# Attention a: another order of the work inside a step, on TensorE first and on the four engines that feed it

## The chip, the cores and the metric

The kernel runs on one core of one Trainium2 chip. The metric is the device time of one execution in microseconds (us). Before the change it is 5544.91 us, the median of three runs (5527.25 to 5550.4).

## The reference, cut to what matters

Four blocks run one after the other on x of shape 32 x 256 x 128: attention a, a mixture of experts, attention b, the mixture of experts again. The change touches attention a alone:

```python
q, k, v = heads of (layernorm(x) @ W_qkv.T + b_qkv)      # 16 heads of 8
scores = q @ k^T * 128 ** -0.5                           # 256 x 256 for each batch and head
masked = the largest 76 scores of each row, -inf elsewhere
out = softmax(masked) @ v
x = x + out @ W_out.T + b_out
```

The top 76 of 256 in each row are the costly part. The kernel finds a threshold for each row: three counting passes over the scores steer a guess to within a few ranks, and a short exact search ends it.

## The kernel before

**Groups and steps.** Attention a handles 64 groups. A group is 8 heads of one batch, so each batch has two. The code issues one `step(t, b, u)` after another (`schedule`, a software pipeline written out by hand): u = t mod 4, an even step is the first of its batch bb = t // 2. The middle of it is a hardware loop (`Fori`) whose body is four steps, so every fourth step ends with the loop's branch. In step t the engines work on different groups:

- TensorE makes the raw scores of group t+1 (`score`, L641, and the first two heads of t+2 at the end, `first_scores`). For groups t-3 and t-2 it makes the transposed scores less the row's maximum (`below_max`, L668), adds a huge negative number where a score is under its threshold (`remove`, L675), and multiplies the exponentials by the values (`weigh`, L689).
- VectorE (DVE) moves the scores from three rotating banks `S` to SBUF, taking the row maximum (`evac`, L961). For group t-1 it takes the sixteen largest values under the upper threshold (`largest`, L976 to L989); for t-2 it picks the threshold (`picks`), checks it (`check_flags`, L1035) and, where a row failed, searches again (`redo`). It normalises the sums (`normalise`, L1025, L1027).
- ScalarE (ACT) counts in three passes of 16 (`count`, L845), takes the exponentials (`exponentials`, L831) from the two banks `PT` to `pT`, and moves projections and sums out of PSUM.
- GpSimd (POOL) moves the guesses between passes (`move`, L479 to L481), computes the scores under the threshold (`outsiders`, `gone`, L493), and two powers (`front`, L453 and L454, and `guess`, L459). SyncE's queue issues the copies and the transposing DMA of each group's negated maxima.

**The order on each queue.** TensorE's step has four parts, d = 0 to 3. Part d handles a pair of heads (`PAIRS`: heads 2,3 then 4,5 then 6,7 of group t-3, then 0,1 of group t-2). `free_bank(t + 1, n + 1)` waits until DVE has evacuated the bank that the next two heads of scores need; then two `below_max`, two `score` and two `remove` are interleaved, twice; then come the projections of the batch ahead, and last `weigh` of the same pair. ACT's step has nine parts, h = 0 to 8, each about five counts; the exponentials of a pair stand ahead of h = 1, 3, 5 and 7. DVE's step has eight parts, one for each head.

**The shared banks.** The projections, the moments, the transposes of the sums and the flags go through two more banks, M0 and M1. `USES` lists the order in which their users take turns, and `m0_before` and `m1_before` turn an entry into a semaphore count: a user waits until the user before it has been read out.

Of the kernel before, what the change touches and what calls it, by code (L numbers as in the profile page):

```python
# [5 lines left out]
P = 128  # L6
# [50 lines left out]
def build(nc, x, W_qkv, b_qkv, W_out, b_out, Wq, Wk, Wv, Wp, pos, gate_w, gate_bias,  # L57
# [7 lines left out]
    with ctx:  # L65
# [307 lines left out]
        def wait(eng, sm, v):  # L373

            if not (isinstance(v, int) and v <= 0):
# [5 lines left out]
        USES = ({"v": 0, "xT": -1, "q0": -1, "q1": -1, "k": -1, "qn": -1, "gram": -1, "qtok": -1, "mom": -1},  # L381
                {"f0": 1, "ktok": -1, "n0": 2, "oT": 2, "f1": 1, "y": 2, "n1": 1})

        def before(m, b, what):

            order = USES[m]
            first = sum(lag == -1 for lag in order.values())
            if not isinstance(b, int):
                return b * len(order) + first - sum(max(lag, 0) for lag in order.values()) + list(order).index(what)
            n = first  # L390
            for c in range(b + 1):
# [26 lines left out]
        PAIRS = ((3, 2), (3, 4), (3, 6), (2, 0))  # L418

# [15 lines left out]
        with nc.Block() as block:  # L435
            @block.gpsimd
            def _(pool):
# [31 lines left out]
                def step(t, b, u):  # L469
# [49 lines left out]
                    if even and runs(bb, 0, BATCH):  # L519
                        wait(pool, s["m0c"], m0_before(bb, "v") + 1)  # L520
# [37 lines left out]
            def _(pe):  # L558
# [43 lines left out]
                def moments(n):  # L602
                    use0(n)
                    for h in range(HALVES):
                        last = nc.tensor.matmul(M0[:, 0:P], ktok[:, h, :], ktok[:, h, :], start=(h == 0), stop=(h == HALVES - 1))
                    last.then_inc(s["m0"], 1)
# [20 lines left out]
                wait(pe, s["m1c"], 1)  # L627
                for n, f in enumerate((moments, q_rows, spreads)):
                    f(5 + n)
# [25 lines left out]
                def step(t, b, u):  # L655
# [23 lines left out]
                    def weigh(g, v, h):  # L679
# [4 lines left out]
                        if h == 0:  # L684
                            wait(pe, s["oc"], g)
                            pe.wait_ge(s["vput"], bb)
# [7 lines left out]
                    def turn_sums():  # L694
                        wait(pe, s["oc"], t - 2)
                        use1(m1_before(bb, "n0" if even else "n1"))
                        for i in range(HALVES):
                            for c in range(2):
                                last = nc.tensor.transpose(M1[:, (i * 2 + c) * P:(i * 2 + c + 1) * P], osum[:, c, i * P:(i + 1) * P], ident[:, :])
                        last.then_inc(s["m1"], 1)  # L700

                    def turn_o():
                        pe.wait_ge(s["on"], 2 * (bb - 1))
                        use1(m1_before(bb, "oT"))
                        for i in range(HALVES):
                            last = nc.tensor.transpose(M1[:, i * P:(i + 1) * P], onrm[:, i, :], ident[:, :])
                        last.then_inc(s["m1"], 1)

                    def project_o():
                        use1(m1_before(bb, "y"))  # L710
# [6 lines left out]
                    for d in range(4):  # L717
# [3 lines left out]
                        ahead = d < 3 and runs(t, -1)  # L721
                        n = 2 * d + 2
                        if ahead:
                            free_bank(t + 1, n + 1)
                        if runs(g):
                            wait(pe, s["turned"], TURNED * (g + 1))
                            wait(pe, s["pt"], 8 * g + a)
                        for k in range(2):
                            if runs(g):
                                below_max(v, a, k)  # L730
                                below_max(v, a + 1, k)
                            if ahead:
# [8 lines left out]
                        if even:  # L741
                            if d == 0 and runs(bb, 0, BATCH):
                                values(m0_before(bb, "v"))
                            if d == 1:
                                if runs(t, 2):
                                    judged()
                                if front:
                                    turn_x(bb + 1, m0_before(bb, "xT"))
                            if d == 2 and front:
                                project(1, m0_before(bb, "q1"))  # L750
                                k_rows(m1_before(bb, "ktok"))
                            if d == 3 and runs(t, 3):
                                turn_sums()
                        else:
                            if d == 0:
                                if tail:
                                    turn_o()
                                if front:
                                    wait(pe, s["m1c"], m1_before(bb, "ktok") + 1)
                                    moments(m0_before(bb, "gram"))  # L760
                            if d == 1:
                                if runs(t, 2):
                                    judged()
                                if front:
                                    spreads(m0_before(bb, "mom"))
                            if d == 2 and tail:
                                project_o()
                            if d == 3 and runs(t, 3):
                                turn_sums()
                        weigh(g, v, a)  # L770
                        if even and front:
                            if d == 1:
                                project(0, m0_before(bb, "q0"))
                            if d == 2:
                                project(2, m0_before(bb, "k"))
                            if d == 3:
                                queries(m0_before(bb, "qn"))
                        if not even and front and d == 0:
                            wait(pe, s["m0c"], m0_before(bb, "qn") + 1)
                            q_rows(m0_before(bb, "qtok"))  # L780
                    if even and front:
                        wait(pe, s["m0c"], m0_before(bb, "k") + 1)
                    if runs(t, -2):
                        first_scores(t + 2, u + 2)
# [4 lines left out]
            def _(act):  # L789
# [32 lines left out]
                take_qn(4)  # L822
                own.end()
# [10 lines left out]
                def step(t, b, u):  # L834
# [18 lines left out]
                    for h in range(9):  # L853
                        if h % 2 == 1:
                            late, a = PAIRS[h // 2]
# [8 lines left out]
                        if h == 0 and even and runs(bb, 0, BATCH):  # L864
                            take_v(bb, m0_before(bb, "v"))
                        if even and front:
# [4 lines left out]
                            if h == 7:  # L871
# [4 lines left out]
                        if not even and h == 1 and runs(bb, 2, BATCH):  # L876
                            wait(act, s["m1"], m1_before(bb, "oT") + 1)
                            nc.scalar.copy(oT[:, :], M1[:, 0:T]).then_inc(s["m1c"], 1)
# [6 lines left out]
            def _(dve):  # L885
# [35 lines left out]
                def take_g(n):  # L921
                    wait(dve, s["m0"], n + 1)
                    V.tensor_tensor(gram[:, :], M0[:, 0:P], mask_bd[:, :, :].rearrange("p h d -> p (h d)"), ALU.mult).then_inc(s["m0c"], 1)

                def take_mom(b, n):
                    wait(dve, s["m0"], n + 1)
                    dve.sem_inc(s["gate"], 1)
                    wait(dve, s["m0c"], n)
# [9 lines left out]
                take_g(5)  # L938
                take_qr(6)
                take_mom(0, 7)  # L940
                own.end()

                def step(t, b, u):
# [76 lines left out]
                    def normalise():  # L1020

                        n1 = m1_before(bb - 1, "n1") if even else m1_before(bb, "n0")
# [21 lines left out]
                    for h in range(8):  # L1044
# [10 lines left out]
                        if h == 0 and runs(t, 4):  # L1055
# [3 lines left out]
                        if front and even and h == 6:  # L1059
                            take_k(m1_before(bb, "ktok"))  # L1060
                        if front and not even:
                            if h == 1:
                                take_g(m0_before(bb, "gram"))
                            if h == 2:
                                take_qr(m0_before(bb, "qtok"))
                            if h == 4:
                                take_mom(bb + 1, m0_before(bb, "mom"))
                        if h == 6 and not even and tail:
# [849 lines left out]
```

## Time and profile before

| | |
|---|---|
| profiled execution | 5548.73 us |
| span of its core | 5547.0 us |
| TensorE (PE) busy | 4738.9 us, 85% |
| weight loads (PEld) busy | 3322.2 us, 60% |
| VectorE (DVE) busy | 4094.9 us, 74% |
| ScalarE (ACT) busy | 3148.7 us, 57% |
| GpSimd (POOL) busy | 2516.4 us, 45% |

Attention a fills about the first 2810 us. Of the 40 slices of the span, the first twenty show a granted TensorE clock of mostly 5 or 6 tenths, the others 9 or more. A row of the waits names the engine and the instruction that stood still, what released it, and then the total, the number of times and the longest. A row of the timeline gives the start, the duration, the engine, the line, what is written and read, how many were merged (x4), and in brackets how long the engine had been idle and what ended that.

### The profile page before, as it was taken

To read this page: it belongs to the slowest core of one execution; us is meant where nothing else is said; L and a number is where in the kernel's file an instruction comes from. 1 tells how busy PE (TensorE), PEld (TensorE's weight loads), DVE (VectorE), ACT (ScalarE), POOL (GpSimd) and SP (SyncE) were. 2 spreads that over 40 slices of the span, in tenths; PEclk is the share of its full clock that TensorE was granted. 3 is DMA by queue.
4 is the path that set the end of the run, shared out by engine and by line. 5 is a ranking of instruction groups with operands and counts; after the bars stand their busy time and mean duration, and the time that the engine had idled before them with its cause. 6 is when DMAs were issued, how large, how long until landed. Compare 5 with 4: busy or idle time off the path is not lost. (4 is left out here: it accounts for less than half of the span.)

```text
span 5547.0 us, 121740 instructions
## 1 busy us (share of the span) xinstructions
PE 4738.9 (85%) x34686; PEld 3322.2 (60%) x34686; DVE 4094.9 (74%) x14487; ACT 3148.7 (57%) x10145; POOL 2516.4 (45%) x3026
## 2 busy tenths in 40 slices
PE   4578788788786887887889999989999998999998
PEld 2244444444443444444468888866666666888887
DVE  3788888888887888888958888855555554788886
ACT  3587777677775777777622222257667776222222
POOL 0465555565554555656644444421111111444444
PEclk6566665565665566667589999999999999999999
DMA  2000000000000000000023443410000000434344
GB/s 67 10 13 10 10 13 10 10 13 9 10 13 7 13 10 10 13 10 12 7 58 81 84 85 81 89 24 10 10 10 12 10 10 9 92 77 91 78 87 98
DMA packets 358589, 188.51 MB, mean 34 GB/s; under 512 B 190691, under 2 KB 346886, under 8 KB 358150
## 3 DMA queue, kind: packets, MB, share of 16 engines
q1 hardware_dynamic: 358150, 183.55, 16.4%
q8 instruction: 167, 2.74, 0.2%
q14 instruction: 272, 2.23, 0.1%
HBM read 147.04 MB, written 11.01 MB: 28 GB/s over the span
## 5 line engine op out<-in xcount | busy, mean ns | idle before, releaser
L845 ACT ACTIVATE junk<-SS,nt 128x256 bf16<-128x256 f32 x3072 | 1515.4, 502 | 188.4 <-POOL nt L481 113.3
L493 POOL TENSOR_SCALAR gone<-SS,mid 128x256 bf16<-128x256 f32 x1024 | 1193.0, 1180 | 664.3 <-DVEq L1039 533.2
L1206 POOL TENSOR_TENSOR f_hid<-f_g_m,f_cbs 128x256 f32<-128x256 f32 x1024 | 743.4, 726 | 853.2 <-DVE f_g_m L1451 660.6
L1306 ACT ACTIVATE f_th<-bank 128x256 f32<-128x256 f32 x1088 | 417.1, 383 | 1149.0 <-PE bank L1237 1149.0
L1236 PE MATMUL bank<-f_xTf,wgT 128*128 128x256 f32 x2176 | 692.3, 400 | 54.3 <-DVE f_g_m L1451 38.6
L668 PE MATMUL bank<-q4x,k4x 32*128 32x256 f32 x2048 | 526.2, 603 | 224.4 <-DVE SS L961 186.9
L1852 DVE TENSOR_REDUCE nmxb<-bank 128x2 f32<-128x512 f32 x512 | 330.1, 688 | 474.6 <-PE bank L1624 474.6
L1237 PE MATMUL bank<-f_xTf,wuT 128*128 128x256 f32 x2176 | 651.5, 381 | 0.0
L1268 PEld LDWEIGHTS bank<-wdT,f_hid 128*128 128x128 f32 x4096 | 601.5, 191 | 66.9 <-POOL f_hid L1206 12.5
L1268 PE MATMUL bank<-wdT,f_hid 128*128 128x128 f32 x4096 | 629.6, 276 | 10.5 <-POOL f_hid L1206 10.4
L845 ACT ACTIVATION_READ_ACCUMULATOR junk<-SS,nt 128x1 f32 x3072 | 599.5, 195 | 0.0
L689 PE MATMUL bank<-pT,vaug 128*32 128x256 f32 x2048 | 436.2, 572 | 136.1 <-ACT pT L831 133.5
L1443 DVE SCALAR_TENSOR_TENSOR f_g_s<-f_th,bank 128x256 f32<-128x256 f32 x1088 | 452.0, 415 | 107.1 <-ACT f_th L1306 87.5
L976 DVE SCALAR_TENSOR_TENSOR zt<-SS,hi_t 128x256 f32<-128x256 f32 x1024 | 481.9, 511 | 59.3 <-issue 28.4
L961 DVE TENSOR_SCALAR_CACHE_REDUCE SS<-bank 128x256 f32<-128x256 f32 x1024 | 386.9, 416 | 170.3 <-PE bank L641 157.8
L1451 DVE TENSOR_TENSOR f_g_m<-f_g_s,bank 128x256 f32<-128x256 f32 x1088 | 457.1, 420 | 74.9 <-DVE f_g_s L1443 3.7
L641 PE MATMUL bank<-k,q 32*128 32x256 f32 x2048 | 465.9, 559 | 30.3 <-DVE SS L961 30.1
L1743 ACT ACTIVATE probb<-bank,nmxb 128x256 f32<-128x256 f32 x1024 | 440.6, 494 | 78.7 <-DVE nmxb L1852 78.7
L668 PEld LDWEIGHTS bank<-q4x,k4x 32*128 32x128 f32 x2048 | 219.7, 261 | 415.5 <-DVE SS L961 236.0
L1553 POOL TENSOR_TENSOR q<-qrow,mask_h 128x1024 f32<-128x1024 f32 x64 | 137.2, 2144 | 715.8 <-DMA qrow<-q_rows 649.6
L1237 PEld LDWEIGHTS bank<-f_xTf,wuT 128*128 128x128 f32 x2176 | 416.3, 191 | 57.3
L831 ACT ACTIVATE pT<-bank 128x512 f32<-128x512 f32 x512 | 276.1, 592 | 277.8 <-PE bank L675 277.7
(233 smaller groups left out, 8134.9 us busy)
## 6 DMA issues: line engine op xcount, KB each, us to landing
f_cbs<-f_shares SPq DMA_DIRECT2D x512, 256.0 KB, 5.8
q4x<-q SPq DMA_DIRECT2D x64, 256.0 KB, 2.3
k4x<-k SPq DMA_DIRECT2D x64, 128.0 KB, 2.1
qrow<-q_rows SPq DMA_DIRECT2D x512, 8.0 KB
q_rows<-qTb SPq DMA_DIRECT2D x32, 128.0 KB, 1.7
out_dram<-xres SPq DMA_DIRECT2D x4, 1024.0 KB, 9.3
q4x<-nmx_rows SPq DMA_DIRECT2D x128, 4.0 KB
f_shares<-f_combT SPq DMA_DIRECT2D x64, 32.0 KB, 1.4
```

What stands on the lines that cost most here:

```text
L493: last = pool.tensor_scalar(gone[:, h % 4, i, :], SS[:, (u - lag) % 4, c, :], mid[:, (u - lag) % 4, c:c + 1], 0.0, ALU.subtract, ALU.min)
L641: last = nc.tensor.matmul(S[h % 3][:, i * T:(i + 1) * T], q4[rows(h), par, 2 * (u % 2) + h // 4, i * P:(i + 1) * P], k4[rows(h), par, u % ...
L668: nc.tensor.matmul(PT[h % 2][:, k * T:(k + 1) * T], k4x[rows(h), v, k * P:(k + 1) * P], q4x[rows(h), v, h // 4, :], start=True, stop=False)
L845: nc.scalar.activation(junk[:, c % 2, :], SS[:, uu % 4, c, :], ACT.Sign, bias=bias(c), accum_out=acc[:, k, uu % 4, c:c + 1]).then_inc(s["s ...
L976: n = own.mark(V.scalar_tensor_tensor(zt[:, i, :], SS[:, z, c, :], hi_t[:, y, c:c + 1], SS[:, z, c, :], ALU.is_le, ALU.mult))
L1206: pool.tensor_tensor(hid[:, e % NBUF, :], g_m[:, e % NBUF, :], cbs[:, par, e, :], ALU.mult).then_inc(s["hid"], 1)
L1236: nc.tensor.matmul(g[:, 0:T], wgT[:, e, :], xTf[:, par, :], start=True, stop=True)
L1237: nc.tensor.matmul(g[:, T:2 * T], wuT[:, e, :], xTf[:, par, :], start=True, stop=True).then_inc(s["gu"], 1)
L1268: last = nc.tensor.matmul(Y[par][h][:, 0:D], src[:, h * P:(h + 1) * P], wdT[:, e, :], start=(e == 0), stop=(e == NBLK - 1))
L1443: n = own.mark(V.scalar_tensor_tensor(g_s[:, e % 3, :], th[:, e % 3, :], 1.0, g[:, 0:T], ALU.add, ALU.mult))
L1451: V.tensor_tensor(g_m[:, e % NBUF if e < EB else NBUF, :], g_s[:, e % 3, :], g[:, T:2 * T], ALU.mult).then_inc(s["gm"], 1)
L1743: last = nc.scalar.activation(probb[:, u % 4, i, :], S[u % 4][:, i * T:(i + 1) * T], ACT.Exp, bias=nmx[:, u % 4, i:i + 1], scale=1.0)
```

## The change

TensorE: in each part d the scores of the next group come first, as four `score` pairs in a row, and `below_max` and `remove` follow by themselves. `weigh` follows another table, `SUMS`, and handles the pair of the part before. `turn_sums` moves from the end of step t to part 0 of the next step. Of the projections, `values` moves from part 0 of the even step to the end of the odd step before, behind `first_scores`; `turn_x` from part 1 to part 0; the moments (`gram`) from part 0 of the odd step to the end of the even one, and to bank M1; `turn_o` from part 0 to part 1, and to bank M0; `queries` goes behind `first_scores`.

ACT: the exponentials stand ahead of h = 2, 4, 6 and 8. The copy of the sums (`osum`) goes from h = 6 to h = 8, `take_qn` from 7 to 8, `take_v` from h = 0 of the even step to h = 8 of the odd one before, `oT` from h = 1 to h = 4.

DVE: `normalise` goes from h = 0 to h = 2, `take_k` from 6 to 7, `take_qr` from 2 to 3, `take_mom` from 4 to 5, the last addition to `xres` from 6 to 7. POOL: `front` stands ahead of `outsiders(3, (6, 7))`.

The core of the diff:

```diff
-        USES = ({"v": 0, "xT": -1, "q0": -1, "q1": -1, "k": -1, "qn": -1, "gram": -1, "qtok": -1, "mom": -1},
-                {"f0": 1, "ktok": -1, "n0": 2, "oT": 2, "f1": 1, "y": 2, "n1": 1})
+        USES = ({"xT": -1, "q0": -1, "q1": -1, "k": -1, "qn": -1, "qtok": -1, "oT": 2, "mom": -1, "v": -1},
+                {"n0": 2, "f0": 1, "ktok": -1, "gram": -1, "n1": 2, "f1": 1, "y": 2})
+        SUMS = ((3, 0), (3, 2), (3, 4), (3, 6))
...
-                    outsiders(3, (6, 7))
                     if even and ahead:
                         front(bb + 1)
+                    outsiders(3, (6, 7))
...
                     def turn_sums():
-                        wait(pe, s["oc"], t - 2)
+                        wait(pe, s["oc"], t - 3)
...
+                        if d < 3 and runs(t, -1):
+                            n = 2 * d + 2
                             free_bank(t + 1, n + 1)
+                            for i in range(HALVES):
+                                score(n, u + 1, i)
+                                score(n + 1, u + 1, i)
+                        if d == 2 and front:
+                            if even:
+                                project(1, m0_before(bb, "q1"))
+                            else:
+                                wait(pe, s["m1c"], m1_before(bb, "gram") + 1)
+                                spreads(m0_before(bb, "mom"))
                         if runs(g):
                             wait(pe, s["turned"], TURNED * (g + 1))
                             wait(pe, s["pt"], 8 * g + a)
-                        for k in range(2):
-                            if runs(g):
+                            for k in range(2):
                                 below_max(v, a, k)
                                 below_max(v, a + 1, k)
-                            if ahead:
-                                score(n, u + 1, k)
-                                score(n + 1, u + 1, k)
-                            if runs(g):
                                 if k == 0:
                                     wait(pe, s["out"], 8 * g + a + 2)
                                 remove(a, k)
                                 remove(a + 1, k)
+                        late, a = SUMS[d]
+                        weigh(t - late, (u - late) % 4, a)
+                        if d == 0:
+                            if runs(t, 4):
+                                turn_sums()
+                            if front and even:
+                                turn_x(bb + 1, m0_before(bb, "xT"))
+                            if front and not even:
+                                q_rows(m0_before(bb, "qtok"))
+                        if d == 1:
+                            if not even and tail:
+                                turn_o()
+                            if runs(t, 2):
+                                judged()
+                            if front and even:
+                                project(0, m0_before(bb, "q0"))
+                        if d == 2:
+                            if front and even:
+                                k_rows(m1_before(bb, "ktok"))
+                                project(2, m0_before(bb, "k"))
+                            if not even and tail:
+                                project_o()
+                        if d == 3:
+                            if even and front:
+                                wait(pe, s["m0c"], m0_before(bb, "k") + 1)
+                            if runs(t, -2):
+                                first_scores(t + 2, u + 2)
+                            if even and front:
+                                moments(m1_before(bb, "gram"))
+                                queries(m0_before(bb, "qn"))
+                            if front and not even:
+                                values(m0_before(bb, "v"))
...
-                        if h % 2 == 1:
-                            late, a = PAIRS[h // 2]
+                        if h >= 2 and h % 2 == 0:
+                            late, a = PAIRS[h // 2 - 1]
                             exponentials(t - late, a)
                             exponentials(t - late, a + 1)
...
-                        if h == 6 and runs(t, 3):
+                        if not even and h == 4 and runs(bb, 2, BATCH):
+                            wait(act, s["m0"], m0_before(bb, "oT") + 1)
+                            nc.scalar.copy(oT[:, :], M0[:, 0:T]).then_inc(s["m0c"], 1)
+                        if not even and front and h == 8:
+                            take_v(bb + 1, m0_before(bb, "v"))
+                        if h == 8 and runs(t, 3):
                             wait(act, s["pv"], 4 * (t - 2))
                             nc.scalar.copy(osum[:, :, :].rearrange("p c i -> p (c i)"), O[:, :]).then_inc(s["oc"], 1)
...
-                        if h == 0 and runs(t, 4):
+                        if h == 2 and runs(t, 4):
                             normalise()
```

## Rows read from the trace of the kernel before

**Rows 1.** The page: TensorE's line of busy time (busy, share, instructions).

```profile
PE 4738.9 (85%) x34686; PEld 3322.2 (60%) x34686; DVE 4094.9 (74%) x14487; ACT 3148.7 (57%) x10145; POOL 2516.4 (45%) x3026
```

**Rows 2.** Windows: 28 steps of attention a; then everything after it.

```profile
456.39:1616.31 1159.92, 936.68 (x4510) 530.72 (x4508) 965.07 (x3753) 851.21 (x3110) 677.63 (x757) 0.62 0.06 11
2800.00:5547.00 2747.00, 2589.64 (x24366) 2106.71 (x24366) 1847.68 (x5768) 1204.20 (x3046) 961.92 (x1281) 0.98 0.27 55
```

**Rows 3.** Waits of TensorE in those 28 steps: total us, times, longest.

```profile
PE bank L668 <- DVE SS L961: 83.6, 55, 7.2
PE bank L689 <- ACT pT L831: 55.9, 42, 2.3
PE bank L699 <- ACT osum L875: 35.9, 18, 3.7
PE bank L668 <- DMA q4x<-nmx_rows: 25.0, 4, 7.0
PE bank L582 <- ACT q L807: 13.3, 11, 2.0
```

**Rows 4.** Waits of VectorE in the same 28 steps.

```profile
DVE SS L961 <- PE bank L641: 73.2, 35, 7.4
DVE stats L896 <- issue: 23.6, 7, 3.5
DVE ktok L915 <- PE bank L599: 20.9, 12, 2.4
DVE xn L910 <- POOL rstd L454: 19.7, 14, 2.0
```

**Rows 5.** Groups by line, same window: busy, mean ns, then idle before by releaser.

```profile
L976 DVE SCALAR_TENSOR_TENSOR zt<-SS,hi_t 128x256 f32<-128x256 f32 x448 | 210.3, 510 | 25.4 <-issue 9.1 <-POOLq L504 8.0 <-DVE flags L1037 7.0
L589 PE MATMUL bank<-bv,ones 1*128 1x128 f32 x56 | 22.2, 497 | 0.0
L588 PE MATMUL bank<-wvT,xT 128*128 128x128 f32 x56 | 21.5, 488 | 0.0
```

**Rows 6.** Timeline, where an even step ends: the first scores, and DVE.

```profile
1042.32 2.08 PE L641 MATMUL bank<-k,q 32*128 32x256 f32 x8
1044.43 0.42 DVE L961 TENSOR_SCALAR_CACHE_REDUCE SS<-bank 128x256 f32<-128x256 f32 x1 [7.38 <-PE bank L641]
```

**Rows 7.** Timeline of TensorE at the end of an odd step.

```profile
1157.88 1.23 PE L668 MATMUL bank<-q4x,k4x 32*128 32x256 f32 x4
...
1161.13 1.10 PE L699 MATMUL bank<-ident,osum 128*128 128x128 f32 x4
1162.38 1.92 PE L689 MATMUL bank<-pT,vaug 128*32 128x256 f32 x8
1164.23 2.08 PE L641 MATMUL bank<-k,q 32*128 32x256 f32 x8
```

**Rows 8.** Timeline of TensorE: the same eight matmuls of `weigh` elsewhere.

```profile
1067.85 1.06 PE L689 MATMUL bank<-pT,vaug 128*32 128x256 f32 x8
```

**Rows 9.** Timeline, part 1 of an odd step and of an even step, up to the flags.

```profile
1060.31 0.21 PE L664 MATMUL bank<-fail,ones 128*1 128x16 f32 x2
1063.32 0.16 DVE L1035 CAST flags<-bank 1x16 int32<-1x16 f32 x1
...
1096.62 0.60 DVE L910 TENSOR_SCALAR xn<-xres,mv,rstd 128x128 f32 x2 [0.80 <-POOL rstd L454]
1097.97 1.22 PE L668 MATMUL bank<-q4x,k4x 32*128 32x256 f32 x4 [0.77 <-DVE SS L961]
1103.06 0.21 PE L664 MATMUL bank<-fail,ones 128*1 128x16 f32 x2
1104.98 0.16 DVE L1035 CAST flags<-bank 1x16 int32<-1x16 f32 x1
```

**Rows 10.** Timeline of POOL over the end of an odd step, and DVE behind it.

```profile
1157.02 0.20 POOL L479 TENSOR_SCALAR shift<-acc 128x16 f32<-128x16 f32 x1 [2.08 <-ACT junk L845]
1174.45 1.10 DVE L976 SCALAR_TENSOR_TENSOR zt<-SS,hi_t 128x256 f32<-128x256 f32 x2 [0.81 <-POOLq L504]
```

More of the change, by code:

```diff
@@ L389, in before @@
                 return b * len(order) + first - sum(max(lag, 0) for lag in order.values()) + list(order).index(what)
-            n = first
-            for c in range(b + 1):
+            n = 0
+            for c in range(-1, b + 1):
                 for o, lag in order.items():
@@ L626, in _ @@
                 k_rows(0)
-                wait(pe, s["m1c"], 1)
-                for n, f in enumerate((moments, q_rows, spreads)):
-                    f(5 + n)
+                q_rows(5)
+                moments(1)
+                wait(pe, s["m1c"], 2)
+                spreads(6)
+                values(7)
                 def rows(h):
@@ L685, in weigh @@
                             wait(pe, s["oc"], g)
-                            pe.wait_ge(s["vput"], bb)
+                            wait(pe, s["vput"], bb - 1 if even else bb)
                         for k in range(HALVES):
@@ L739, in step @@
                                 remove(a + 1, k)
-                        if even:
-                            if d == 0 and runs(bb, 0, BATCH):
-                                values(m0_before(bb, "v"))
[L744 to L784, printed above, removed]
+                        late, a = SUMS[d]
[7 more added lines that the diff above has]
+                                q_rows(m0_before(bb, "qtok"))
@@ L822, in _ @@
                 take_qn(4)
+                take_v(0, 7)
                 own.end()
@@ L870, in step @@
                                 take_q(h - 4, bb + 1, (par + 1) % 2, m0_before(bb, ("q0", "q1", "k")[h - 4]))
-                            if h == 7:
+                            if h == 8:
                                 take_qn(m0_before(bb, "qn"))
-                        if h == 6 and runs(t, 3):
+                        if not even and h == 4 and runs(bb, 2, BATCH):
[4 more added lines that the diff above has]
+                        if h == 8 and runs(t, 3):
                             wait(act, s["pv"], 4 * (t - 2))
                             nc.scalar.copy(osum[:, :, :].rearrange("p c i -> p (c i)"), O[:, :]).then_inc(s["oc"], 1)
-                        if not even and h == 1 and runs(bb, 2, BATCH):
-                            wait(act, s["m1"], m1_before(bb, "oT") + 1)
-                            nc.scalar.copy(oT[:, :], M1[:, 0:T]).then_inc(s["m1c"], 1)
                     if u == 3:
@@ L1020, in normalise @@
                     def normalise():
-                        n1 = m1_before(bb - 1, "n1") if even else m1_before(bb, "n0")
+                        n1 = m1_before(bb, "n0" if even else "n1")
                         wait(dve, s["m1"], n1 + 1)
@@ L1058, in step @@
                             check_flags()
-                        if front and even and h == 6:
+                        if front and even and h == 7:
                             take_k(m1_before(bb, "ktok"))
@@ L1062, in step @@
                             if h == 1:
-                                take_g(m0_before(bb, "gram"))
-                            if h == 2:
+                                take_g(m1_before(bb, "gram"))
+                            if h == 3:
                                 take_qr(m0_before(bb, "qtok"))
-                            if h == 4:
-                                take_mom(bb + 1, m0_before(bb, "mom"))
-                        if h == 6 and not even and tail:
+                            if h == 5:
+                                take_mom(bb + 1, m0_before(bb, "mom"), m0_before(bb, "qtok") + 1)
+                        if h == 7 and not even and tail:
                             wait(dve, s["m1"], m1_before(bb, "y") + 1)
```

34 lines of the change are left out of this document (15 added, 19 removed).

## The prediction

> **What bounds the kernel now.** I read the page first: no engine is full, TensorE is busy for 85% of the span and DVE for 74% [rows 1]. The windows split that in two. After attention a TensorE is busy for 2590 of 2747 us at a granted clock of 0.98; the change touches nothing there and I leave it alone. In attention a it is busy for 81% at 0.62, and DVE for 83% [rows 2]. So attention a is a loop in which two nearly equal engines take turns in waiting for each other.
>
> I count in steps. The 28 steps of the window take 1159.92 us, 41.43 us each. TensorE is busy for 936.68 / 28 = 33.45 us of a step and idle for 7.98; DVE is busy for 34.47 and idle for 6.96 [rows 2].
>
> The waits say what for. TensorE, per step: 83.6 + 25.0 = 108.6 us or 3.9 for DVE to free a score bank (I put the four waits named after the DMA of the maxima here as well: at 7.0 us they are the length of the 7.2 that stands under DVE, they come at the loop's branch, and a group's maxima are not needed before its third step), 2.0 for exponentials ahead of `weigh`, 1.3 for the copy of the sums, 0.5 for a projection to be taken [rows 3]. DVE, per step: 2.6 for raw scores, 0.75 for the k rows, 0.7 for `rstd`, 0.3 for POOL's thresholds (8.0 / 28); the rest is its own, above all the loop's branch (up to 3.5 us each, 0.84 per step) and the flag's load and branch [rows 4, 5].
>
> The timeline shows the worst place. At the end of an even step DVE stands still for 7.38 us until `first_scores` has run [rows 6]; in the code the sums, `weigh` and the queries stand ahead of it on TensorE's queue. The start of the next step's scores waits behind work that is not urgent.
>
> **The change, part by part, per step, on TensorE's queue.**
>
> 1. `weigh` one pair later. Its exponentials are then a whole part old, and ACT has finished them long before. The 2.0 us go. What could be late is the first `weigh`, which now waits for the copy of the sums at the very end of ACT's step; it stands some 7 us into TensorE's step (scores 2.08, a pair 3.25, and what is in front), while ACT's copy follows the end of TensorE's last work by two short copies. I cost it at nothing; if that slack is used up, the wait of point 2 is back, 1.3 us (bounds 0 to 1.3).
>
> 2. `turn_sums` a step on. Its 1.3 us wait goes: the first `weigh` ahead of it has already waited for the same copy. Work unchanged (1.10 us) [rows 7].
>
> 3. The projections in part 2. `project(1)` moves ahead of the pair, so that the pair and a `weigh` stand between it and `project(2)`; ACT's exponentials no longer stand ahead of its copy of q1. The 0.5 us go. Bounds: 0 to 0.5.
>
> 4. `values` at the end of the odd step. The same work, 43.7 us in 28 steps [rows 5], about 3.1 us a time at the lower clock. Every fourth step TensorE idles for 7.0 to 7.2 us over the loop's branch [rows 3]; there it is free, -3.1 / 4 = -0.8 per step. Elsewhere it costs the same at its new place. Bounds: 0 to -0.8; I take -0.8, since the gap is twice as long.
>
> 5. Scores first. DVE gets them about 2 us after the bank is free instead of 5; that takes DVE's waits inside the step. But TensorE loses by it. A pair alone takes 1161.13 - 1157.88 = 3.25 us and eight scores 2.08, together 5.33 [rows 7], while interleaved they take 1103.06 - 1097.97 = 5.09 [rows 9]. That is +0.24 three times, +0.7 per step. Bounds 0 to 1.0.
>
> 6. `first_scores` ahead of queries and moments, and no sums ahead of it. It starts earlier by the 1.10 us of the sums, by the queries and by the waits of points 2 and 3. This costs TensorE nothing and is what lets DVE run.
>
> TensorE's step is then 41.43 - 2.0 - 1.3 - 0.5 - 0.8 + 0.7 = 37.5 us, its 3.1 us of remaining waits for banks still counted.
>
> **The same on DVE.** What I take as gone: 2.6 for scores; 0.75 for the k rows, taken one part later; 0.7 for `rstd`, because POOL's `front` no longer stands behind a round of `gone`. 41.43 - 2.6 - 0.75 - 0.7 = 37.4 us. `turn_x` now needs `xn` in part 0. `xn` ended at 1097.2 and the next part began at 1097.97, when a bank came free [rows 9]; TensorE waits there anyway, so nothing. The 0.3 us for the thresholds stay about as they are: POOL's chain in an odd step (flags, rounds of `gone`, the powers of `guess`) ended 0.81 us after DVE's need; the wait of 2.08 us for the second count goes, since the exponentials now stand behind that count, but `normalise` no longer delays DVE ahead of it [rows 10]. So DVE's floor is 37.4, and 37.1 without that wait.
>
> **The new wait.** The flags. `judged` ran 3.0 us (odd) and 1.9 us (even) before DVE read it [rows 9]. Now 1.92 us of `weigh` stand ahead of it [rows 7], in odd steps also `turn_o` (0.6), and 0.24 from point 5: +2.2 even, +2.8 odd. DVE arrives 0.55 later, because `normalise` now stands at h = 2. Where part 1 starts on DVE's freeing of a bank, as it does here, that fits with 0.3 to 0.8 us left. Where TensorE is behind and does not wait for that bank, the whole delay falls on DVE: up to 3 us, and POOL's `gone` waits behind the flags too. Bounds 0 to 3; I take 1.1, as part of the steps is of each kind. TensorE's 37.5 and DVE's 37.4 are the same within what I can tell; with 1.1 on top the step is 38.6 us.
>
> POOL, ACT and SyncE's queue get no new work; ACT is busy for 851 of 1160 us [rows 2], and its copies (`take_v`, `take_qn`) wait at the step's end for the last of TensorE's work, which costs the ten spare us it has. The few steps that fill and drain the pipeline, and the two searches again that the data force, stay: I count 60 of the 64 steps at the new pace.
>
> (41.43 - 38.6) x 60 = 170 us. The profiled execution took 5548.7 us (1.7 around its span), 3.8 above the median of the runs. 5548.7 - 170 = 5379; I say 5380.
>
> **What the clock does to it.** The same eight matmuls of `weigh` take 1.92 us at the low level and 1.06 at the high [rows 7, 8]: a factor of 0.55. A mean of 0.62 means that the clock is at 2.4 GHz for 0.24 of the time, so 33.45 us of busy time would be 33.45 / (1 - 0.45 x 0.24) = 37.5 at 1.2 GHz throughout. The sum above leaves the 0.24 as it is. TensorE at 81% busy has 0.62, at 94% busy it has 0.98 [rows 2].
>
> The Trainium skill, "TensorE: Matmul & The Clock Gate", Part 1 (The HAM clock gate), says that the throttled state is the default and activity releases it. By that rule the change is worth more than the sum, because it closes gaps; the rows of this case at least do not speak against it.
>
> **The rivals.**
>
> *DVE becomes the bound.* With gaps gone the clock's share at 2.4 GHz rises from 0.24 to, say, 0.5; busy falls to 37.5 x 0.775 = 29.1 us, TensorE's sum to 33.1, and DVE's 37.2 decides, with no wait for flags. 4.2 x 60 = 252: 5295 us. For: [rows 2]. Against: TensorE's durations were those of the low level through 8 us with hardly a gap [rows 7]. 0.17. This is also where the rule of the Trainium skill's clock page would lead.
>
> *The flags take the place.* The full 3 us in each step: 40.5 us, 55 us gained: 5490. For: TensorE has no slack in even steps. Against: it waited for a bank, 0.77 us, right ahead of part 1 [rows 9]. 0.12.
>
> *Nothing moves.* TensorE's queue is only work at the low clock, and its waits for DVE grow by what the others lose: 5545. Against: 7.38 us of DVE's idleness stand right behind work that moves away [rows 6]. 0.05.
>
> *Slower: the clock falls.* The full-width work is regrouped, blocks of eight scores stand alone, and the level stays at 1.2 GHz: 37.5 instead of 33.45, 38.6 + 4.05 = 42.65 us a step, +1.2 x 60: 5620. It decides from a mean clock of about 0.54 downwards, where the 2.8 us gained are used up. Against: fewer gaps. 0.07.
>
> **How the numbers follow.** The forecast, 38.6 give or take 1 us a step (5320 to 5440), has 0.59. The range of 8 in 10 takes in most of DVE's bound below and the late flags above: 5285 to 5490. A measurement can't tell less than about 0.5% (28 us) from no change. Faster by more than that: 0.59 + 0.17 + nearly all of 0.12, 0.87; within 0.5%: 0.06; slower: 0.07.
>
> **What would show it.** Right: DVE's wait for L641 and TensorE's for L831 and L875 nearly gone; the 28 steps at about 1080 us; a wait of DVE at L1035 for L664, new, about 1 us a step; granted clock 0.60 to 0.70. Wrong, if DVE still waits several us at the first scores of an odd step (then point 6 has failed), if TensorE waits in part 0 for L875 (point 1), or if the clock of attention a is below 0.55.

## The result, and the profile after

The changed kernel takes 5298.69 us (median of four runs, 5298.19 to 5302.46); the kernel before took 5547.65 us (four runs, 5527.25 to 5553.43). The ratio is 0.9559, with a 95% interval from 0.9534 to 0.9584: 249 us less. Forecast were 5380 us, with a range from 5285 to 5490.

The windows of the kernel after: 28 steps of attention a, the same ones as in [rows 2], then everything behind it. Columns as there.

```profile
434.26:1475.68 1041.42, 921.10 (x4508) 510.72 (x4508) 964.16 (x3753) 853.19 (x3109) 680.28 (x757) 0.64 0.07 12
2560.00:5300.00 2740.00, 2586.66 (x24348) 2105.07 (x24344) 1846.32 (x5768) 1205.77 (x3044) 963.89 (x1280) 0.98 0.27 55
```

A step takes 1041.42 / 28 = 37.19 us instead of 41.43. The work is what it was: DVE is busy for 964.2 us (965.1 before), TensorE for 921.1 (936.7). DVE is now busy for 93% of the time, TensorE for 88%, and the granted clock has moved from 0.62 to 0.64 only. From the 4th to the 64th step, counted by the writes of `nmx`, it is 2286.7 us instead of 2517.2: 230.5 of the 246.3 us between the two spans; some 4 lie before and some 11 behind.

The waits of the same 28 steps after, DVE first, then TensorE (total, times, longest):

```profile
DVE stats L895 <- issue: 27.6, 7, 4.0
DVE zt L975 <- issue: 18.2, 14, 1.3
DVE zt L975 <- DVE flags L1036: 13.9, 14, 1.0
DVE SS L960 <- PE bank L644: 1.5, 4, 0.8
DVE flags L1034 <- PE bank L667: 0.9, 4, 0.3
```

```profile
PE bank L644 <- DVE SS L960: 82.9, 54, 6.2
PE bank L575 <- DVE xn L909: 25.8, 14, 5.3
PE bank L702 <- DVE gram L922: 6.5, 4, 2.0
PE bank L583 <- ACT q L805: 4.4, 7, 0.8
```

Against [rows 3, 4]: DVE's 73.2 us for scores are 1.5; those for the k rows and for `rstd` are gone from the list. What is left to it is its own, 59.7 us of branch and flags. TensorE's waits for exponentials (55.9) and for the copy of the sums (35.9) are gone, and so is the wait named after the DMA of the maxima (25.0). Nearly all that it still waits for is DVE: 115.2 us, 4.1 a step. Of these, 25.8 us are a new wait: `turn_x` for `xn`, at the start of each even step.

The flags, in the same two rows as in [rows 9], in an odd and in an even step of the kernel after:

```profile
1123.74 0.21 PE L667 MATMUL bank<-fail,ones 128*1 128x16 f32 x2
1124.25 0.16 DVE L1034 CAST flags<-bank 1x16 int32<-1x16 f32 x1
...
1162.34 0.21 PE L667 MATMUL bank<-fail,ones 128*1 128x16 f32 x2
1165.63 0.16 DVE L1034 CAST flags<-bank 1x16 int32<-1x16 f32 x1
```

From the end of `judged` to DVE's reading it is 0.30 us in the odd step and 3.08 in the even one, where [rows 9] have 2.80 and 1.71. In the 14 odd steps of the window `judged` starts 0 to 2.0 us before DVE reads, and in four of them DVE waits, 0.9 us in all; in the even ones it starts 2.4 to 4.4 us before. So in odd steps most of the slack is used up by what now stands ahead of the flags, and in even steps it has grown.

### The profile page after: what moved, and what is told of

It reads as the page before. It is cut to its first block and busy times, and to the rows that moved or that the text cites. A ratio compares the mean times of both kernels' runs of the same rounds, so it can differ in the third digit from the quotient of the medians.

```text
span 5300.7 us, 121671 instructions
## 1 busy us (share of the span) xinstructions
PE 4709.3 (89%) x34686; PEld 3284.1 (62%) x34686; DVE 4089.0 (77%) x14487; ACT 3157.1 (60%) x10145; POOL 2522.7 (48%) x3026
## 5 line engine op out<-in xcount | busy, mean ns | idle before, releaser
L644 PE MATMUL bank<-k,q 32*128 32x256 f32 x2048 | 452.7, 574 | 220.0 <-DVE SS L960 216.6
L644 PEld LDWEIGHTS bank<-k,q 32*128 32x128 f32 x2048 | 264.2, 270 | 348.1 <-DVE SS L960 280.7
L692 PE MATMUL bank<-pT,vaug 128*32 128x256 f32 x2048 | 425.5, 559 | 0.7 <-issue 0.6
L984 DVE MATCH_REPLACE8 zt<-L,zt 128x256 f32<-128x256 f32 x1024 | 409.0, 405 | 0.0
```

Of the source, the lines that this page charges most:

```text
L644: last = nc.tensor.matmul(S[h % 3][:, i * T:(i + 1) * T], q4[rows(h), par, 2 * (u % 2) + h // 4, i * P:(i + 1) * P], k4[rows(h), par, u % ...
```

## The experiments

"Per step" is over the same 28 steps, "60 steps" from the 4th to the 64th, both from the profiled execution. The ratio is to the runs of the kernel before on the same chip, which itself took from 5548 to 5568 us there; so I compare ratios with 0.9559, not medians. The middle columns come from one execution each, on several chips. Those 20 us of the kernel before would be about 0.3 us a step, if all of them lay in attention a; a difference of 0.3 to 0.6 us in "per step" alone is therefore weak, and I say in each such case what the ratio and the waits show. Every edit is to the kernel after, unless it says "before". Each expectation names two theories, A and B, and the time that each would give.

| | ratio (95%) | per step | 60 steps | clock | TensorE busy per step |
|---|---|---|---|---|---|
| before | 1 | 41.43 | 2517.2 | 0.62 | 33.45 |
| after | 0.9559 (0.9534 to 0.9584) | 37.19 | 2286.7 | 0.64 | 32.90 |
| interleaved | 0.9578 (0.9562 to 0.9594) | 37.75 | 2316.2 | 0.65 | 31.88 |
| sums with their pair | 1.0145 (1.0122 to 1.0167) | 43.09 | 2621.6 | 0.55 | 36.27 |
| first scores last | 0.9573 (0.9552 to 0.9595) | 37.65 | 2314.8 | 0.64 | 32.62 |
| flags late | 0.9569 (0.9553 to 0.9585) | 37.54 | 2305.1 | 0.64 | 32.78 |
| before, first scores early | 0.9997 (0.9981 to 1.0012) | 41.18 | 2515.2 | 0.66 | 31.60 |
| front late | 0.9662 (0.9631 to 0.9692) | 38.40 | 2356.1 | 0.64 | 33.14 |
| more TensorE | 0.9580 (0.9550 to 0.9610) | 37.55 | 2317.8 | 0.69 | 32.68 |
| before, more TensorE | 1.0108 (1.0072 to 1.0144) | 42.76 | 2595.2 | 0.63 | 35.48 |
| sums and exponentials old | 1.0134 (1.0111 to 1.0157) | 42.90 | 2607.8 | 0.55 | 36.87 |
| exponentials early | 1.0005 (0.9988 to 1.0022) | 41.55 | 2540.2 | 0.60 | 34.63 |
| more VectorE | 1.0118 (1.0095 to 1.0141) | 40.00 | 2451.5 | 0.61 | 34.33 |
| 28 steps in the body | 0.9465 (0.9447 to 0.9484) | 36.39 | 2237.8 | 0.65 | 32.58 |

**Is VectorE the bound?** More work on VectorE:

```diff
                         evac(h)
+                        own.link(V.tensor_copy(spare[:, h % 4, :], ident[:, :]))
```

> The changed kernel with more work on VectorE: behind each of the eight evacuations one more copy of 128x128 to a spare buffer, waited for by VectorE itself; about 0.3 us each, 2.4 us a step. Theory A (VectorE is the bound): the full added time, 2 to 3 us a step, 5420 to 5480 us, and TensorE's waits for banks longer by it. Theory B (the step is held by another ring, through TensorE or POOL): under 1 us a step, 5300 to 5360 us.

```profile
454.01:1574.11 1120.10, 961.34 (x4508) 533.32 (x4508) 1027.15 (x3976) 855.25 (x3109) 682.59 (x757) 0.61 0.06 11
```

(The window of its 28 steps.) DVE's busy time grew by (1027.15 - 964.16) / 28 = 2.25 us a step, and it waits for each copy itself; the step grew by 2.81, and TensorE's wait for banks from 82.9 to 113.7 us. All of it shows, and in attention a that is 165 us. Theory A. The median rose by more, since a further 146 us appeared behind attention a, where nothing was edited; see the end.

**Has TensorE slack, and had it before?** More work on TensorE, after and before (the first time, `below_max` closes its own accumulation):

```diff
                             for k in range(2):
+                                if d in (0, 2):
+                                    below_max(v, a, k, True)
+                                    below_max(v, a + 1, k, True)
                                 below_max(v, a, k)
```

> The changed kernel with more work on TensorE: below_max is made twice in parts 0 and 2, the first time for nothing; 8 more matmuls, 1.2 us at the high clock to 2.1 us at the low, in each step. Theory A (TensorE has 3 us of slack in a step, VectorE binds): 0 to 0.5 us a step, 5300 to 5330 us. Theory B (TensorE's work is a bound as well): the full 1.2 to 2.1 us, 5370 to 5420 us.

> The same on the kernel before: 8 more matmuls on TensorE in each step, 1.2 to 2.1 us. Theory A (before, TensorE's queue set the pace through VectorE's wait for the scores): nearly all of it, 1.2 to 2.1 us a step, 5620 to 5670 us. Theory B (it had slack there too): under 0.5 us a step, 5550 to 5575 us.

The windows of the two, after and before:

```profile
435.82:1487.19 1051.37, 915.08 (x4960) 534.01 (x4958) 961.72 (x3753) 852.14 (x3110) 679.84 (x758) 0.69 0.07 12
```

```profile
462.77:1660.08 1197.31, 993.35 (x4967) 585.83 (x4966) 967.27 (x3753) 853.25 (x3113) 676.82 (x758) 0.63 0.06 10
```

The edit adds eight matmuls a step, and each stands in the trace as two records (4960 against 4508 in 28 steps). After, the step grows by 0.36 us, as A said, and the ratio's interval overlaps that of the kernel after. What does come is in DVE's waits:

```profile
DVE SS L963 <- PE bank L644: 8.3, 7, 1.4
DVE zt L978 <- POOLq L505: 5.9, 7, 0.8
```

Before, TensorE's busy time grows by 2.03 us a step and the step by 1.33 (A said 1.2 to 2.1). So the pace of before went through TensorE. For the kernel after the test is weaker than it was meant to be: TensorE's busy time did not grow, it fell from 921.1 to 915.1 us, because the granted clock rose from 0.64 to 0.69. It shows that this work is nearly free there, not that two more busy microseconds would be. That TensorE has slack rests on its waits for DVE, 4.1 us a step, and on the test of DVE above.

**Which part of the change brings it?** Five parts were undone singly, and the flags were put later than in either kernel. Interleaved again (the four `score` lines go back between `below_max` and `remove`; with that `project(1)` and `spreads` of part 2, which stood between the scores and the pair, come behind the pair, as they did before):

> The changed kernel, with below_max, score and remove of parts 0 to 2 interleaved again as before; all else stays. Theory A (VectorE is now the bound, at 37.2 us a step, and TensorE has about 3 us of slack in each step, so that scores 3 us later still come in time): no change, 5285 to 5330 us, VectorE's wait for L644 under 0.5 us a step. Theory B (scores first is what feeds VectorE): the wait inside the step that the trace of before showed, 1.4 us, is back, 0.5 to 1.4 us a step on about 59 steps: 5330 to 5380 us.

0.56 us a step, which is in B's range; 0.0019 in the ratio, and the two intervals overlap. The waits decide against B: DVE does not wait for L644 at all. It has another wait that the kernel after lacks, for the product that `spreads` makes, and this is 0.44 of the 0.56 us:

```profile
DVE prod L931 <- PE bank L619: 12.3, 13, 1.2
```

So what little is lost comes with the place of `spreads`, not with scores that are too late. TensorE's busy time falls by 921.1 - 892.6 = 28.5 us, 1.0 us a step, at a clock of 0.65 instead of 0.64: that is about what the separate blocks cost it (how much of it is the clock was not taken apart), and it is paid out of slack.

First scores last:

```diff
-                            if runs(t, -2):
-                                first_scores(t + 2, u + 2)
                             if even and front:
                                 moments(m1_before(bb, "gram"))
                                 queries(m0_before(bb, "qn"))
                             if front and not even:
                                 values(m0_before(bb, "v"))
+                            if runs(t, -2):
+                                first_scores(t + 2, u + 2)
```

> The changed kernel, with moments and queries (even step) and values (odd step) ahead of first_scores instead of behind it. Theory A (the place of first_scores is what took away VectorE's wait at the head of a step; 1.3 to 2.3 us of work come ahead of it in even steps, 1.8 to 3.1 us in odd ones): 0.5 to 2 us a step, 5330 to 5420 us, all of it as VectorE's wait for L644. Theory B (removing the other waits was enough): 5290 to 5315 us.

And the same move made alone, on the kernel before (`first_scores`, with its wait for k, directly behind the last `remove` of part 3):

> The kernel before, with one thing moved: first_scores directly behind the last pair of a step, ahead of the sums, weigh and queries. Theory A (the 2.6 us a step that VectorE waited for scores were a matter of what stood ahead of first_scores): about half of the gain, 1.5 to 2.5 us a step, 5400 to 5460 us. Theory B (TensorE was bound by its own work and its waits for the exponentials; the order only moves the wait): 5520 to 5555 us.

After, 0.46 us a step, DVE waiting 13.4 us for L644 in 28 steps instead of 1.5: the mechanism of A, just under the low edge of its size, and the ratio does not tell it from no change. Before, it changes nothing, B. The waits of that kernel, TensorE and DVE, say why:

```profile
PE bank L689 <- ACT pT L832: 95.3, 42, 4.0
PE bank L641 <- DVE SS L962: 85.3, 14, 6.7
DVE qtok L920 <- PE bank L612: 38.8, 14, 3.1
DVE SS L962 <- PE bank L641: 19.2, 20, 3.3
```

DVE's wait for scores does fall, from 73.2 to 19.2 us. But the first scores, now early on TensorE's queue, wait there for DVE to free their bank (L641, 85.3 us in 14 steps), TensorE also stands longer ahead of `weigh` (95.3 against 55.9), and what it makes behind both comes later: DVE waits 38.8 us for the q rows instead. The 7.38 us that I had read as the worst place [rows 6] was the place where the delay came out, not where it arose.

Sums with their pair:

```diff
-        SUMS = ((3, 0), (3, 2), (3, 4), (3, 6))
+        SUMS = PAIRS
...
-                            wait(pe, s["vput"], bb - 1 if even else bb)
+                            wait(pe, s["vput"], bb)
...
-                        if h == 8 and runs(t, 3):
+                        if h == 7 and runs(t, 3):
                             wait(act, s["pv"], 4 * (t - 2))
```

> The changed kernel, with weigh again handling the pair of its own part (and the copy of the sums at h = 7 instead of 8, which this needs). Theory A (TensorE's waits for exponentials were 2.0 us a step; they come back, and though TensorE has 3 us of slack on average, the sums and the flags behind them have none): 0.5 to 2 us a step, 5330 to 5420 us, with waits of TensorE for the exponentials and of VectorE for the flags. Theory B (these waits fit wholly into TensorE's slack): 5290 to 5315 us.

```profile
PE bank L692 <- ACT pT L830: 190.7, 112, 4.8
DVE SS L960 <- PE bank L644: 68.0, 21, 6.7
DVE rinv L1024 <- PE bank L702: 48.6, 28, 2.7
DVE flags L1034 <- PE bank L667: 43.9, 26, 2.8
```

```profile
455.17:1661.69 1206.52, 1015.60 (x4485) 565.47 (x4486) 968.42 (x3752) 853.69 (x3098) 667.16 (x755) 0.55 0.06 10
```

(Waits, then the window.) Undoing this one thing costs 5.9 us a step, more than the whole gain of 4.24, so the kernel is slower than the one before the change. Both expectations were far too low. TensorE waits for exponentials ahead of each of the 112 `weigh`, 190.7 / 28 = 6.8 us a step, and the sums, the flags and the scores behind it are late. The granted clock falls to 0.55, and with it the same matmuls take 36.3 us a step instead of 32.9. Busy time and this wait make up the whole step, 36.3 + 6.8 = 43.1: here TensorE is the bound. How much of the 5.9 us is the wait and how much the clock was not taken apart.

Was that only because the exponentials had moved too? Both tables as before, and the copy of the sums at h = 6 (of the edit, only what is new is shown):

```diff
-                        if h >= 2 and h % 2 == 0:
-                            late, a = PAIRS[h // 2 - 1]
+                        if h % 2 == 1:
+                            late, a = PAIRS[h // 2]
```

> The changed kernel, with weigh in the part of its own pair and also the exponentials back ahead of h = 1, 3, 5 and 7 and the copy of the sums at h = 6: both tables as before, the rest of the change stays. Weigh back alone had cost 335 us over 60 steps, with the clock at 0.55. Theory A (what cost so much was weigh behind exponentials that had moved a ninth of a step later, together): waits of TensorE for exponentials of about 2 us a step as before the change, 38.5 to 40 us a step, 5380 to 5480 us. Theory B (weigh in the part of its own pair alone is what holds the step, wherever the exponentials are): 41 us or more, 5520 us or more.

42.90 us a step, clock 0.55: B. In this order, with the scores first, a `weigh` behind its own exponentials holds the step at either place of the exponentials. And the exponentials alone, by the same edit to ScalarE, with `weigh` left a pair later:

> The changed kernel, with only the exponentials back ahead of h = 1, 3, 5 and 7. Theory A (with weigh a pair later, ScalarE has slack and VectorE binds): ScalarE waits longer for TensorE, the guesses come later, 0 to 0.5 us a step, 5300 to 5330 us. Theory B (ScalarE standing still for a pair delays the counts, and through POOL the thresholds and VectorE): 0.5 to 2 us a step, 5330 to 5420 us.

Neither theory by its size: the whole gain is gone, 41.55 us a step. The mechanism of B is there, DVE waits 33.9 us for POOL's thresholds and did not after, but it is the smaller part. ScalarE waits for the pairs for 252.1 us in 28 steps, 9.0 a step, where it is 85.7 after and 112.3 before:

```profile
ACT pT L830 <- PE bank L678: 252.1, 84, 5.4
DVE SS L960 <- PE bank L644: 70.8, 13, 7.2
PE bank L575 <- DVE xn L909: 56.3, 14, 7.9
PE bank L583 <- ACT q L805: 51.4, 28, 3.2
DVE zt L975 <- POOLq L505: 33.9, 10, 5.2
```

One even step of it, in time, shows the way through all three engines:

```profile
1025.68 0.61 PE L678 MATMUL bank<-steep,gone 128*128 128x128 bf16 x4
1026.19 1.08 ACT L830 ACTIVATE pT<-bank 128x512 f32<-128x512 f32 x2 [5.42 <-PE bank L678]
1029.62 0.82 ACT L805 ACTIVATE q<-bank,bqs 128x256 f32<-128x256 f32 x2
1030.49 2.08 PE L583 MATMUL bank<-xTc,wksT 128*128 128x256 f32 x4 [1.20 <-ACT q L805]
1037.74 2.08 PE L644 MATMUL bank<-k,q 32*128 32x256 f32 x8
1039.85 0.42 DVE L960 TENSOR_SCALAR_CACHE_REDUCE SS<-bank 128x256 f32<-128x256 f32 x1 [7.20 <-PE bank L644]
```

ScalarE stands for 5.42 us ahead of the exponentials, since TensorE now makes scores and a projection before the pair. Its counts and the copy of q1 stand behind them on its queue, TensorE's `project(2)` waits for that copy, the first scores are behind that, and DVE stands for 7.20 us. With the exponentials one part later the counts and the copy run in that gap: TensorE's wait for q1 is then 4.4 us in 28 steps instead of 51.4.

Front late, and flags late:

```diff
+                    outsiders(3, (6, 7))
                     if even and ahead:
                         front(bb + 1)
-                    outsiders(3, (6, 7))
```

> The changed kernel, with POOL's front behind outsiders(3, (6, 7)) again. Theory A (turn_x on TensorE now needs xn in part 0, and rstd comes some 5 us later): VectorE waits 1 to 3 us for rstd in even steps, TensorE for xn, 0.5 to 1.5 us a step: 5330 to 5390 us. Theory B (only the 0.7 us a step of before come back): 5335 us. Nothing, 5300 us, if VectorE is not the bound.

```diff
-                            if runs(t, 2):
-                                judged()
                             if front and even:
                                 project(0, m0_before(bb, "q0"))
+                            if runs(t, 2):
+                                judged()
```

> The changed kernel, with judged behind project(0) in even steps, 1.1 us later at the high clock and 2.1 us at the low. In the trace after the change the flags came 0.03 to 1.8 us after they landed in half of the steps, 2 to 4 us in the others. Theory A (that slack is used up in even steps): VectorE waits for the flags 0.8 to 2 us in every even step, 5320 to 5355 us. Theory B (TensorE is early enough): 5290 to 5315 us.

Front late costs 1.21 us a step and 0.0103 in the ratio, A: DVE waits 30.3 us for `rstd` (2.2 in each even step) and TensorE 55.1 for `xn`. Flags late costs 0.35 us a step and DVE waits 11.7 us for L667 in 17 of 28 steps, where there were 0.9 us in 4: the mechanism of A, at half its size, but the difference of the ratios, 0.0010, is inside the intervals.

**What is left.** Every fourth step of the kernel after is 4.0 us longer than the others. 28 steps in the body of the loop:

```diff
-            with eng.Fori(*BODY) as i:
-                for u in range(4):
-                    step(i * 4 + u, i * 2 + u // 2, u)
+            with eng.Fori(0, 2) as i:
+                for w in range(7):
+                    for u in range(4):
+                        step(i * 28 + 4 * (w + 1) + u, i * 14 + 2 * (w + 1) + u // 2, u)
```

> The changed kernel with 28 steps instead of four in the body of the hardware loop, so that its branch comes twice instead of 14 times. In the trace VectorE, now the bound, idles 4.0 us at each branch, and every fourth step is 4.0 us longer. Theory A (that is the branch): 12 x 4.0 = 48 us less, 5245 to 5265 us. Theory B (it is the clearing of the engine's own semaphore at every fourth step, or the longer program has to be fetched at the same cost): 5290 to 5310 us.

```profile
429.56:1448.46 1018.90, 912.36 (x4508) 506.73 (x4508) 964.80 (x3753) 851.64 (x3109) 679.00 (x757) 0.65 0.07 13
```

```profile
DVE stats L896 <- issue: 3.9, 1, 3.9
```

(The window of its 28 steps, and DVE's wait at the loop's branch.) 2237.8 us for 60 steps, 48.9 less, and one idle stretch of 3.9 us in 28 steps instead of seven: 12 x 4.07. It is the branch, not the clearing of the semaphore, which is still there at every fourth step. With 5257.55 us, a ratio of 0.9465, this is faster than the kernel after. The Trainium skill, "Runtime: NRT & Kernel Launch", Instruction fetch mechanics, says that a taken branch whose target is outside the engine's small instruction window forces a fetch before the engine goes on. The runs agree that the branch is dear, 4.07 us for a body of four steps; that the fetch is what takes the time, no run here shows.

## Why the prediction was right, and where it was not

The direction and the range held, but the time is that of the rival "DVE becomes the bound" (5295, a chance of 0.17), not that of the forecast (5380): the gain is 249 us, where 170 were forecast. By the steps of the prediction:

- Points 1 and 2, the waits for exponentials and sums: right. 55.9 and 35.9 us became nothing, and the new wait for the copy at the end of ScalarE's step does not show. But they were costed as two terms of a sum, 3.3 us. Undoing point 1 costs 5.9 us a step: everything behind the waiting `weigh` is late too, and the clock falls.
- Point 3: right, 13.3 us became 4.4. It was named as a side effect, 0.5 us; but without the exponentials' move, to which it belongs, the whole gain is lost (4.4 us a step when undone).
- Point 4, `values` at the branch: not tried alone. TensorE still waits 1.7 to 2.2 us behind each branch, and 6.2 once; with DVE as the bound, slack on TensorE is worth nothing, so the 0.8 us counted for it are not shown by any run.
- Point 5: +0.7 us of TensorE's time forecast, 1.0 measured. Right in kind, and it costs nothing, for the same reason. What it was to bring, DVE's scores in time inside the step, is not shown: with the scores interleaved DVE did not wait for them either.
- Point 6, the place of `first_scores`: right that DVE's wait would go, wrong on the cause. Alone it is worth nothing before, and at most 0.46 us after.
- `turn_x` in part 0 was to cost TensorE nothing, because it waited for a bank there anyway. It now waits 25.8 us for `xn` in 14 even steps; that too is paid out of slack.
- DVE's floor: 37.4, and 37.1 without POOL's wait. Measured 37.19. This was the best number in the text. The wait for POOL was forecast to stay, and it is gone.
- **The step that failed** is the new wait for the flags, 1.1 us a step: 0.9 / 28 = 0.03 measured. The working next to it holds for odd steps (0.8 us left; `judged` starts half a microsecond early in the median); for even steps it had 0.3 us left, and 2.4 to 4.4 are there. What was wrong is the guess that TensorE would often be behind: it waits for DVE for 4.1 us a step. The guess came from its sum of 37.5, in which 3.1 us of waits for banks were left standing as though they were work. They are slack: TensorE's own sum is 34.4 (37.5 - 3.1), well below DVE's. 37.4 in place of 38.6 is 4.0 us a step, 242 us, 5307.
- The rival's reason did not hold either: the clock was to rise to 0.75 and went to 0.64. DVE became the bound without it.
- The slower rival, a falling clock, did not come in the kernel as changed; it is what one sees at 0.55 when `weigh` stands behind its own exponentials.

By the Trainium skill, "TensorE: Matmul & The Clock Gate", Part 1, activity releases the throttle. The runs agree only in part: the clock is 0.69 where work was added, but 0.55 where TensorE idles for 6.8 us a step and 0.62 before, where it idles for 7.98. Idle time alone does not order them. Nor did work without gaps bring the clock up, as this stretch of the kernel before shows, TensorE busy for 17.85 of 18.00 us at a granted clock of 0.50:

```profile
1148.30:1166.30 18.00, 17.85 (x76) 9.68 (x76) 15.97 (x63) 14.46 (x54) 13.78 (x12) 0.50 0.07 23
```

## What to carry to other kernels

When in-order engines feed each other, a wait is worth more than its length: add the busy time and the waits that an engine owes to nobody for each engine, take the largest as the floor, and do not count waits for the other engine as work. Test the place where a stall shows by moving the thing alone; here that gave nothing. What the gain could not do without are two moves that let each engine have other work between a request and its answer: with all the rest changed, neither of them gives 42.90 us a step, the later exponentials alone 43.09, the later `weigh` alone 41.55, and both 37.19. Whether the two would do as much on the kernel before, without the rest, was not tried.

## What was not expected of the hardware

- Work added to TensorE made its busy time fall, from 921.1 to 915.1 us in 28 steps, with 452 more records of matmuls: the granted clock rose from 0.64 to 0.69.
- TensorE stayed at the lower clock level, 0.50, through 18 us in which it was busy for 17.85; why is open.
- The loop's branch costs DVE about 4.0 us each time, in a step of 36.
- With eight more instructions a step on VectorE in attention a, the part behind the 64th step took 2979.6 us instead of 2833.1; in the other thirteen traces it is 2830 to 2849. The group of `f_g_s` in the experts' blocks, after and in that kernel, has the same busy time and a new idle time named "issue":

```profile
L1442 DVE SCALAR_TENSOR_TENSOR f_g_s<-f_th,bank 128x256 f32<-128x256 f32 x1088 | 451.3, 415 | 107.1 <-ACT f_th L1305 87.5
```

```profile
L1444 DVE SCALAR_TENSOR_TENSOR f_g_s<-f_th,bank 128x256 f32<-128x256 f32 x1088 | 451.1, 415 | 228.1 <-ACT f_th L1307 107.9 <-issue 100.8 <-DVE f_comb L1401 19.3
```

Why is open; it was not tried. The rule of the Trainium skill on branches, cited above, would be a reason, if the longer program moves a loop across the edge of the window; no run shows it, and with 28 steps in the body, a much longer program, the part behind takes 2839.1 us. What the run does show is that an edit in one loop can be followed by a slower loop later in the program; a verdict on one stage should be read from that stage.
